# Two-layer AdaLN network on one core: the third sequence's rotary projections moved from attention groups 0 to 2 into the lead-in

## The chip, the core and the metric

The kernel runs on one core of one Trainium2 chip. The metric is device time in microseconds (us) of one execution. The engines are TensorE (PE, matmul; PEld is its weight load), VectorE (DVE), ScalarE (ACT), GpSimd (POOL) and SyncE (SP), which only issues DMAs here. Each engine works through its own instructions in order and waits on semaphores.

## What is computed

Four sequences of 512 tokens and 128 channels pass two AdaLN layers. Layer 0 is a Mamba-2 mixer and a dense run of 8 experts; layer 1 is causal attention with rotary positions and a routed MLP with the chosen expert of each token. The change touches the attention of layer 1 alone, which is, cut to what matters:

```python
q = (x @ W_q.T).reshape(B, S, 16, 8).transpose(0, 2, 1, 3)   # B = 4 sequences (two of them in name), S = 512
k = (x @ W_k.T).reshape(B, S, 16, 8).transpose(0, 2, 1, 3)
v = (x @ W_v.T).reshape(B, S, 16, 8).transpose(0, 2, 1, 3)
q, k = apply_rope(q), apply_rope(k)      # o1 = x1*cos - x2*sin, o2 = x1*sin + x2*cos
scores = einsum('bhqd,bhkd->bhqk', q, k) / sqrt(8)
probs = softmax(where(causal, scores, -inf))
attn = einsum('bhqk,bhkd->bhqd', probs, v)
x = x + ga * (attn @ W_o.T)
```

## The kernel before

**Projections.** For sequence b four projections are made, j = 0 to 3: q, q with neighbouring channels swapped, k, and k swapped. `project(b, j)` is one float32 product over the 512 tokens on PE, which the profile shows as two MATMULs of line 1876. `rope(b, j)` multiplies its result by cosine or sine on DVE (line 1309). `rotate` on POOL (line 560) adds two of these to a rotated q or k. ACT and POOL then split it into three bfloat16 parts (`part_hi` and `part_mid`, lines 869 and 873; `rest` and `last_part`, lines 566 and 571). SP stores the parts in DRAM (`parts_out`, line 366) and reads them back in another layout (`relayout`, line 378).

**Groups.** Attention runs over 16 groups of 4 heads, numbered by `it`, four groups to a sequence. Each group has 8 slots, i = 0 to 7. Work is staged: while group `it` makes its transposed scores (`scores_T`, lines 1973 and 1978), its exponentials on ACT (`probs`, line 882) and its weighted values (`weighted_values`, line 1992), the same slots make the plain scores of group `it + 2` on PE (`scores`, line 1900), of which DVE takes row maxima (`maximum`, line 1332). In slot 3 the maxima of group `it + 1`, split into parts by POOL (`max_parts`, lines 610 to 616), are transposed (`maxima_T`, line 1957), copied by ACT (line 967) and put into rows of `qaug` by four DMAs on SP (line 437); `scores_T` of the next group waits for these.

**The lead-in.** The loop begins with `it = -1`, which has no transposed scores and no exponentials: PE makes only plain scores of group 1 and, in slot 3, the maxima's transposes for group 0. Group 0 also carries the last residual of layer 0 and its statistics (lines 1910, 1315, 475 and 480) and a layer norm on DVE (line 494); group 1 carries four transposes for it (`x3_T`, line 1917).

**The ring.** Plain scores, projections and the small transposes share three PSUM banks in turn, in the order in which PE makes them. Before PE writes a bank it waits until the reader of what stood there three items earlier (DVE, or ACT) is done. The order is built by the same loop as PE's and DVE's programs, so a projection that moves takes its place in the ring with it.

The table `ROPE_AT` gives the group in whose slots each projection stands; `ropes_at` adds the slot. Sequence 2's projections are first needed by POOL's `rotate` in group 1.

Of the kernel before, what the change touches and what calls it, by code (L numbers as in the profile page):

```python
# [72 lines left out]
def adaln_kernel(nc, x_in, mod_in, mixw_in, moe0_in, attn_in, moe1_in, const_in, bconst_in, kones_in, out):  # L73
    with ExitStack() as ctx:
# [203 lines left out]
                units.append(parts)  # L278
                maxima_done.append(maxima_done[-1] + len(parts))

        ROPE_AT = {(2, 0): 0, (2, 1): 1, (2, 2): 2, (2, 3): 2, (3, 0): 4, (3, 1): 5, (3, 2): 6, (3, 3): 6}

        def ropes_at(it, i):

            return [bj for bj, at_it in ROPE_AT.items() if at_it == it and i == (1 if bj[1] == 2 else 5)]

        def parts_at(it):

# [24 lines left out]
        for it in range(-1, 16):  # L313
            for i in range(8):
                if it + 2 < 16:
                    for n in at_slot[i]:
                        ring.append((("mx", it + 2, n), ("mx", 16 * (it + 2) + maxima_done[n + 1])))
                if i == 3 and 0 <= it + 1 < 16:
                    ring.append((("mT", it + 1), ("mT", it + 2)))
                if i == 3 and 0 <= it - 1:  # L320
                    ring.append((("oT", it - 1), ("at", it)))
                if i == 5 and it >= 4 and it % 4 == 0:
                    ring.append((("aT", it // 4 - 1), ("aT", it // 4)))
                if i == 7 and it >= 4 and it % 4 == 0:
                    ring.append((("ao", it // 4 - 1), ("x3", it // 4)))
                for b, j in ropes_at(it, i):
                    ring_projection(b, j)
                if it in (4, 8) and i == 6:
                    ring_projection((it + 4) // 4, 4)
                if (it, i) == (0, 1):  # L330
                    ring.append((("y0T", B - 1), ("x2", B)))
                if (it, i) == (1, 1):
                    ring.append((("x3T", B - 1), ("hT", 3 * B)))
                if (it, i) in ROUTER_AT:
                    what = ROUTER_AT[it, i]
                    ring.append((what, {"h4T": ("hT", 3 * B + what[1] + 1), "logits": ("logits", what[1] + 1),
                                        "ranks": ("ranks", what[1] + 1)}[what[0]]))
# [663 lines left out]
        def _(v):  # L1001
# [513 lines left out]
            for it in range(-1, 16):  # L1515
                for i in range(8):
                    if (it, i) == (0, 3):
                        residual(B - 1)
                    if (it, i) == (0, 7):
                        ln_apply(v, 3, x, xn, B - 1)  # L1520
                    if it + 2 < 16:
                        for u in at_slot[i]:
                            maximum(it + 2, u)
                    if i == 3 and 0 <= it - 1:
                        o_norm(it - 1)
                    if i == 7 and it >= 4 and it % 4 == 0:
                        attn_out(it // 4 - 1)
                    for b, j in ropes_at(it, i):
                        rope(b, j)
                    if it >= 5 and it % 4 == 1 and i in (2, 4):  # L1530
                        router_input(it // 4 - 1, i // 2 - 1)
                    if (it, i) == (14, 5):
                        logits_in(0)
                        choose(0)
                    elif (it, i) == (14, 7):
                        positions(0)
                        second_best(0)
                    elif (it, i) == (15, 4):
                        logits_in(1)
                        choose(1)  # L1540
                    elif (it, i) == (15, 7):
                        positions(1)
                        early_table()
                        second_best(1)
# [90 lines left out]
        def _(pe):  # L1635
# [412 lines left out]
            for it in range(-1, 16):  # L2048
                if it == 0:
                    pe.wait_ge(sem("pr"), DENSE)  # L2050
                for i in range(8):
                    if it + 2 < 16:
                        for u in at_slot[i]:
                            scores(it + 2, u)
                    if 0 <= it < 16:
                        scores_T(8 * it + i)
                    if i == 3 and 0 <= it + 1 < 16:
                        maxima_T(it + 1)
                    if i % 2 == 1 and 0 <= 4 * it + i // 2 - 1 < 64:
                        weighted_values(4 * it + i // 2 - 1)  # L2060
                    if i == 3 and 0 <= it - 1:
                        o_T(it - 1)
                    if i == 5 and it >= 4 and it % 4 == 0:
                        a_T(it // 4 - 1)
                    if i == 7 and it >= 4 and it % 4 == 0:
                        attn_out(it // 4 - 1)
                    for b, j in ropes_at(it, i):
                        project(b, j)
                    if it in (4, 8) and i == 6:
                        project_values((it + 4) // 4)  # L2070
                    if (it, i) == (0, 1):
                        y0_T(B - 1)
                    if (it, i) == (1, 1):
                        x3_T(B - 1)
                    if (it, i) in ROUTER_AT:
                        what, n = ROUTER_AT[it, i]
                        router_step[what](n)
# [172 lines left out]
```

## Time and profile before

| | us |
|---|---|
| median of 3 runs | 541.46 (540.17 to 542.07) |
| the profiled execution | 538.46 |
| its span, first to last instruction | 536.5 |
| PE busy | 455.4 (85%) |
| DVE busy | 396.8 (74%) |
| ACT busy | 280.6 (52%) |
| mean granted TensorE clock | 0.927 |

The profiled execution's own time is 3.00 us under the median and 1.96 us over its span. The granted clock is given as a share of full speed: 1.00 is 2.4 GHz and 0.50 is 1.2 GHz. Attention takes the stretch from about 287 us to 444 us of the span.

### The profile page before, as it was taken

What the parts mean: (1) busy time and instruction counts of PE and PEld (TensorE: products, weight loads), DVE (VectorE), ACT (ScalarE), POOL (GpSimd) and SP (SyncE); (2) the same over time, 40 slices, a digit from 0 to 9 for tenths busy, and PEclk for the clock granted to TensorE, in tenths of its full rate; (3) what the DMA queues carried; (4) which work ended last, traced back from release to release, by engine and by line L of the source; (5) the groups of instructions that cost most, each with busy time, mean ns of one, the idle gap of its engine ahead of it and who ended that gap; (6) DMA issues with size and microseconds to landing.
All of it is one profiled execution on the core that took longest, in us unless ns stands there. A gap on an engine that the chain in (4) does not pass through costs nothing.

```text
span 536.5 us, 10400 instructions
## 1 busy us (share of the span) xinstructions
PE 455.4 (85%) x3156; PEld 275.7 (51%) x3156; DVE 396.8 (74%) x1328; ACT 280.6 (52%) x525; POOL 235.6 (44%) x332
## 2 busy tenths in 40 slices
PE   4798778987898999979996899999999997588990
PEld 4664557765653444435332344534545453587990
DVE  5899848889535689778898789888899636445544
ACT  3569986653443444443542578677678753112330
POOL 4210048999300387765843124034065536032760
PEclk9989899999789899989997799999999978579996
DMA  8991000000001532247760003214255101112115
GB/s 350 360 384 37 1 1 2 1 2 0 9 0 53 109 105 84 68 136 197 207 146 2 3 4 90 62 33 135 78 168 182 62 17 46 26 48 74 53 45 166
DMA packets 31471, 47.58 MB, mean 89 GB/s; under 512 B 3709, under 2 KB 21437, under 8 KB 30509
## 3 DMA queue, kind: packets, MB, share of 16 engines
q1 hardware_dynamic: 29448, 43.99, 27.0%
q0 software_dynamic: 1248, 2.59, 1.5%
q8 instruction: 27, 0.44, 0.4%
q10 hardware_dynamic: 720, 0.34, 0.3%
q14 instruction: 28, 0.22, 0.1%
HBM read 27.59 MB, written 19.12 MB: 87 GB/s over the span
## 4 chain that ended last, share of the span: by engine, by line
PE 44%; DVE 16%; issue 9%; POOL 5%; DMA 5%; SPq 4%; ACT 3%; DVEq 0%; POOLq 0%; ACTq 0%
PE ps L1992 6%; DVE arena L1332 4%; PE ps L1928 3%; PE ps L2098 3%; PE ps L1930 3%; PE ps L1876 3%; PE ps L2107 3%; PE ps L1865 3%; PE ps L1978 3%; PE ps L1900 2%; PE ps L1791 2%; DMA arena<-expert_weights 2%; PE ps L1973 1%; DVE arena L1301 1%; POOL slots_x L674 1%
## 5 line engine op out<-in xcount | busy, mean ns | idle before, releaser
L1332 DVE CUSTOM_DVE_ANT_0 arena<-ps,const 128x512 bf16<-128x512 f32 (+3 forms) x256 | 110.8, 486 | 7.7 <-PE ps L1900 7.4
L882 ACT ACTIVATE arena<-ps 128x256 f32<-128x256 f32 (+3 forms) x128 | 85.2, 703 | 38.5 <-PE ps L1978 37.8
L592 POOL TENSOR_TENSOR arena<-arena 128x512 f32<-128x512 f32 x32 | 45.7, 1428 | 63.4 <-DVE arena L1301 63.3
L1900 PE MATMUL ps<-arena 48*128 48x128 bf16 (+3 forms) x256 | 51.6, 310 | 8.8 <-DVE arena L1332 6.6
L1992 PE MATMUL ps<-arena 128*32 128x512 f32 (+3 forms) x512 | 51.0, 464 | 0.4 <-ACT arena L882 0.4
L1978 PE MATMUL ps<-arena 51*128 51x128 bf16 (+3 forms) x256 | 49.0, 310 | 0.0
L1973 PE MATMUL ps<-bconst 64*128 64x64 bf16 x512 | 42.9, 195 | 2.0 <-DMA arena<-arena 1.9
L1900 PEld LDWEIGHTS ps<-arena 48*128 48x128 bf16 x256 | 17.1, 95 | 53.2 <-DVE arena L1332 31.0
L909 ACT ACTIVATE arena<-arena 128x512 f32<-128x512 f32 x32 | 20.1, 629 | 43.8 <-DVE arena L1301 43.0
L1928 PE MATMUL ps<-arena,moe 128*128 128x512 f32 x64 | 35.8, 642 | 5.7 <-DVE arena L1284 5.6
L952 ACT ACTIVATE arena<-ps 128x512 f32<-128x512 f32 x23 | 13.7, 598 | 45.4 <-PE ps L2098 45.4
L1973 PEld LDWEIGHTS ps<-bconst 64*128 64x128 bf16 x512 | 29.4, 97 | 11.2 <-DMA arena<-arena 3.0
L1930 PE MATMUL ps<-arena,moe 128*128 128x512 f32 x64 | 34.2, 618 | 0.0
L682 POOL DMA_INDIRECT tokens_y<-arena,token_at x23 | 22.5, 980 | 26.4 <-DVE token_at L1563 16.1
L1111 DVE SCALAR_TENSOR_TENSOR arena<-ps,mixw,arena 128x511 f32<-128x511 f32 (+2 forms) x48 | 33.1, 740 | 0.9 <-ACT arena L752 0.9
L1865 PE MATMUL ps<-arena,moe 128*128 128x512 f32 x64 | 32.8, 594 | 0.0
L1284 DVE TENSOR_TENSOR arena<-hT,arena 128x512 f32<-128x512 f32 x32 | 24.8, 774 | 9.7 <-DMA arena<-expert_weights 9.7
L1292 DVE SCALAR_TENSOR_TENSOR arena<-ps,moe,arena 128x512 f32<-128x512 f32 x32 | 23.9, 747 | 9.7 <-PE ps L1930 9.3
L2098 PE MATMUL ps<-arena 128*128 128x128 f32 x184 | 27.0, 294 | 3.0 <-DVE arena L1556 2.5
L529 POOL TENSOR_TENSOR arena<-arena 128x256 f32<-128x256 f32 x16 | 12.4, 774 | 37.0 <-ACT arena L745 33.3
L674 POOL DMA_INDIRECT slots_x<-rows,posu x16 | 15.8, 988 | 27.9 <-DVE posu L1445 20.9
L2107 PE MATMUL ps<-arena 128*128 x184 | 26.5, 293 | 0.0
(268 smaller groups left out, 1081.6 us busy)
## 6 DMA issues: line engine op xcount, KB each, us to landing
slots_x<-arena SPq DMA_DIRECT2D x1, 8910.0 KB, 39.4
arena<-expert_weights SPq DMA_DIRECT2D x32, 256.0 KB, 4.0
qk_parts<-arena SPq DMA_DIRECT2D x48, 128.0 KB, 2.4
arena<-qk_parts SPq DMA_DIRECT2D x52, 96.0 KB, 2.4
arena<-moe_in SPq DMA_DIRECT2D x4, 1025.0 KB, 5.4
moe<-moe_in SPq DMA_DIRECT2D x1, 1936.0 KB, 14.2
arena<-slots_x SPq DMA_DIRECT2D x18, 66.0 KB, 1.9
arena<-qk_parts SPq DMA_DIRECT2D x4, 288.0 KB, 5.8
```

Source lines behind the costliest of these rows:

```text
L592: pool.tensor_tensor(yacc[:, ts], yacc[:, ts], pr[:, i % 2, :], ALU.add).then_inc(sem("yacc"), 1)
L882: act.activation(pt[:, u % 4, :, 0:n], ps[:, 4 + 2 * k:6 + 2 * k, 0:n], ACT.Exp, scale=ATT_SCALE).then_inc(sem("probs"), 1)
L1332: v.tensor_tensor_reduce(out=junk[:, done % 2, 0:n], in0=ps[:, k, col:col + n], in1=w["mask"][:, (3 - qt) * P:4 * P], scale=1.0, scalar=3 ...
L1865: pe.matmul(ps[:, 6 + i % 2, :], w["w2"][:, e * D:(e + 1) * D], gT[:, i % 2, :], start=True, stop=True).then_inc(sem("p2_ps"), 1)
L1900: mm = pe.matmul(ps[:, k, col:col + n], qaug[lo:lo + KR, b % 2, 2 * g + j // 2, qt * P:(qt + 1) * P], kaug[lo:lo + KR, b % 2, 2 * g + j // ...
L1928: pe.matmul(ps[:, 2 + i % 2, :], w["w1"][:, e * D:(e + 1) * D], xm[:, i % 2, :], start=True, stop=True).then_inc(sem("p1_ps"), 1)
L1930: pe.matmul(ps[:, 4 + i % 2, :], w["w3"][:, e * D:(e + 1) * D], xm[:, i % 2, :], start=True, stop=True).then_inc(sem("p3_ps"), 1)
L1973: pe.matmul(ps[:, bank, HALF * qh:HALF * (qh + 1)], w["causal"][lo:lo + HALF, qh * P:(qh + 1) * P], w["half"][lo:lo + HALF, :], start=(qh ...
L1978: mm = pe.matmul(ps[:, bank, 0:n], kaug[lo:lo + KM, b % 2, 2 * g + jp, kt * P:(kt + 1) * P], qaug[lo:lo + KM, b % 2, 2 * g + jp, kt * P:S] ...
L1992: mm = pe.matmul(ps[32 * j:32 * j + 32, 3, kt * P:S], va[:, b % 2, kt, 4 * (s % QG) + j, :], pt[:, (2 * m + j // 2) % 4, j % 2, 0:n], star ...
L2098: mm = pe.matmul(ps[:, 4 + n % 2, q * P:(q + 1) * P], w1[:, n % 2, q * P:(q + 1) * P], xT[:, n % 2, :], start=True, stop=True)
L2107: mm = pe.matmul(ps[:, 6 + n % 2, 0:D], gs[:, n % 2, q * P:(q + 1) * P], w["W2"][:, bass.ds(at_w[n] + q * D, D)], start=(q == 0), stop=(q ...
```

## The change

Sequence 2's four projections and the four DVE operations that read them move to `it = -1`, to slots 4, 5, 6 and 7 behind that slot's plain scores. Sequence 3's stay in groups 4 to 6. No instruction is added or removed.

```diff
--- before.py
+++ after.py
@@ -278,11 +278,11 @@
                 units.append(parts)
                 maxima_done.append(maxima_done[-1] + len(parts))
 
-        ROPE_AT = {(2, 0): 0, (2, 1): 1, (2, 2): 2, (2, 3): 2, (3, 0): 4, (3, 1): 5, (3, 2): 6, (3, 3): 6}
+        ROPE_AT = {(2, 0): -1, (2, 1): -1, (2, 2): -1, (2, 3): -1, (3, 0): 4, (3, 1): 5, (3, 2): 6, (3, 3): 6}
 
         def ropes_at(it, i):
 
-            return [bj for bj, at_it in ROPE_AT.items() if at_it == it and i == (1 if bj[1] == 2 else 5)]
+            return [bj for bj, at_it in ROPE_AT.items() if at_it == it and i == (bj[1] + 4 if it < 0 else 1 if bj[1] == 2 else 5)]
 
         def parts_at(it):
 
```

**PE, the lead-in.** The rows start with the four transposes of the maxima (line 1957, slot 3 of `it = -1`). The rows of line 1900 are plain scores, of line 1876 the projection, and lines 1973 and 1978 are the first transposed scores of group 0. Before:

```order
L1957 MATMUL ps<-bconst,arena 12x128 x4
L1900 MATMUL ps<-arena 128x256 x4
L1900 MATMUL ps<-arena 128x512 x2
L1900 MATMUL ps<-arena 128x384
L1900 MATMUL ps<-arena 128x128
L1900 MATMUL ps<-arena 128x384
L1900 MATMUL ps<-arena 128x128
L1900 MATMUL ps<-arena 128x512
L1973 MATMUL ps<-bconst 128x64 x4
L1978 MATMUL ps<-arena 128x128 x2
```

Now:

```order
L1957 MATMUL ps<-bconst,arena 12x128 x4
L1900 MATMUL ps<-arena 128x256 x2
L1876 MATMUL ps<-hT,attn 128x512
L1900 MATMUL ps<-arena 128x256 x2
L1876 MATMUL ps<-hT,attn 128x512
L1900 MATMUL ps<-arena 128x512 x2
L1876 MATMUL ps<-hT,attn 128x512
L1900 MATMUL ps<-arena 128x384
L1900 MATMUL ps<-arena 128x128
L1900 MATMUL ps<-arena 128x384
L1900 MATMUL ps<-arena 128x128
L1876 MATMUL ps<-hT,attn 128x512
```

A projection now stands behind each of the four slots' plain scores, and all four stand ahead of group 0's first `scores_T`.

**DVE, the lead-in.** The rows start at slot 5; line 1332 is the row maximum, in two instructions, and line 1309 the multiplication by cosine or sine. Before:

```order
L1332 ISA arena<-ps,const 128x256
L1332 ISA arena 128x1
L1332 ISA arena<-ps,const 128x256
L1332 ISA arena 128x1
L1332 ISA arena<-ps,const 128x512
L1332 ISA arena 128x1
L1332 ISA arena<-ps,const 128x512
L1332 ISA arena 128x1
L1332 ISA arena<-ps,const 128x384
L1332 ISA arena 128x1
L1332 ISA arena<-ps,const 128x128
```

Now:

```order
L1309 TENSOR_TENSOR arena<-ps,const 128x512
L1332 ISA arena<-ps,const 128x256
L1332 ISA arena 128x1
L1332 ISA arena<-ps,const 128x256
L1332 ISA arena 128x1
L1309 TENSOR_TENSOR arena<-ps,const 128x512
L1332 ISA arena<-ps,const 128x512
L1332 ISA arena 128x1
L1332 ISA arena<-ps,const 128x512
L1332 ISA arena 128x1
L1309 TENSOR_TENSOR arena<-ps,const 128x512
L1332 ISA arena<-ps,const 128x384
```

Each multiplication stands between the maxima of one slot and those of the next.

**PE, from slot 7 of group 1 to slot 2 of group 2.** Lines 1973 and 1978 are transposed scores, line 1992 the weighted values (the row with 384 columns is slot 7's, the one with 512 columns slot 1's). Before:

```order
L1973 MATMUL ps<-bconst 128x64 x4
L1978 MATMUL ps<-arena 128x512 x2
L1992 MATMUL ps<-arena 32x384 x4
L1900 MATMUL ps<-arena 128x512
L1973 MATMUL ps<-bconst 128x64 x4
L1978 MATMUL ps<-arena 128x128 x2
L1900 MATMUL ps<-arena 128x512
L1973 MATMUL ps<-bconst 128x64 x4
L1978 MATMUL ps<-arena 128x128 x2
L1992 MATMUL ps<-arena 32x512 x4
L1876 MATMUL ps<-hT,attn 128x512
L1900 MATMUL ps<-arena 128x384
```

Now:

```order
L1973 MATMUL ps<-bconst 128x64 x4
L1978 MATMUL ps<-arena 128x512 x2
L1992 MATMUL ps<-arena 32x384 x4
L1900 MATMUL ps<-arena 128x512
L1973 MATMUL ps<-bconst 128x64 x4
L1978 MATMUL ps<-arena 128x128 x2
L1900 MATMUL ps<-arena 128x512
L1973 MATMUL ps<-bconst 128x64 x4
L1978 MATMUL ps<-arena 128x128 x2
L1992 MATMUL ps<-arena 32x512 x4
L1900 MATMUL ps<-arena 128x384
```

The projection behind slot 1's weighted values is gone. The other three leave the same kind of gap: one in slot 5 of each of the groups 0, 1 and 2. The rows around them keep their order. ACT's, POOL's and SP's programs keep their order.

## Rows read from the trace of the kernel before

**Rows 1.** The page: busy time, share of the span, instructions.

```profile
PE 455.4 (85%) x3156; PEld 275.7 (51%) x3156; DVE 396.8 (74%) x1328; ACT 280.6 (52%) x525; POOL 235.6 (44%) x332
```

**Rows 2.** Windows from slot 2 to the next group's slot 1: groups 1, 2, 3.

```profile
core 0: us, PE busy (x) PEld busy (x) DVE busy (x) ACT busy (x) POOL busy (x), PEclk, DMA share, GB/s
...
306.97:316.62 9.65, 9.07 (x111) 4.31 (x111) 8.25 (x36) 6.98 (x11) 2.33 (x7) 1.00 0.01 3
316.62:326.85 10.23, 9.65 (x112) 4.20 (x112) 8.59 (x37) 7.40 (x12) 4.42 (x8) 1.00 0.24 64
326.85:334.61 7.76, 7.54 (x107) 3.69 (x108) 7.42 (x36) 7.04 (x12) 3.23 (x7) 1.00 0.23 63
```

**Rows 3.** Timeline of PE, 305 to 312 us.

```profile
305.90 1.07 PE L1992 MATMUL ps<-arena 128*32 128x512 f32 x8
306.89 0.66 PE L1917 MATMUL ps<-const,rows 128*128 128x128 f32 x4
```

**Rows 4.** Timeline of PE, 315 to 335 us.

```profile
315.56 1.06 PE L1992 MATMUL ps<-arena 128*32 128x512 f32 x8
316.55 1.13 PE L1876 MATMUL ps<-hT,attn 128*128 128x512 f32 x2
...
321.26 1.12 PE L1876 MATMUL ps<-hT,attn 128*128 128x512 f32 x2
...
333.54 1.07 PE L1992 MATMUL ps<-arena 128*32 128x512 f32 x8
```

**Rows 5.** Timeline of PE around the lead-in's end; idle time in brackets.

```profile
287.00 0.40 PE L1900 MATMUL ps<-arena 48*128 48x256 bf16 x4
287.74 3.10 PE L1900 MATMUL ps<-arena 48*128 48x512 bf16 x7 [0.35 <-ACT arena L967]
291.79 0.29 PE L1973 MATMUL ps<-bconst 64*128 64x64 bf16 x4 [0.95 <-DMA arena<-arena]
```

**Rows 6.** Timeline of DVE in the lead-in and group 0.

```profile
287.43 0.42 DVE L1332 CUSTOM_DVE_ANT_0 arena<-ps,const 128x256 bf16<-128x256 f32 x1 [0.57 <-PE ps L1900]
...
291.47 0.69 DVE L1332 CUSTOM_DVE_ANT_0 arena<-ps,const 128x512 bf16<-128x512 f32 x1
...
301.79 0.69 DVE L1309 TENSOR_TENSOR arena<-ps,const 128x512 f32<-128x512 f32 x1 [2.52 <-PE ps L1876]
```

**Rows 7.** Chain that ended last: start, us, what.

```profile
289.99 1.75 DMA arena<-arena
...
299.89 1.87 PE ps L1876 x2
```

**Rows 8.** Busy time and granted clock in windows of 1 us, 287 to 302.

```profile
287.00:288.00 1.00, 0.65 (x7) 0.20 (x5) 0.57 (x3) 0.88 (x2) 0.00 (x0) 0.91 0.00 0
...
291.00:292.00 1.00, 0.21 (x8) 0.21 (x10) 1.00 (x5) 0.00 (x0) 0.34 (x2) 0.50 0.03 11
...
295.00:296.00 1.00, 0.27 (x4) 0.07 (x2) 0.96 (x5) 0.87 (x2) 0.00 (x0) 0.50 0.00 0
...
300.00:301.00 1.00, 1.00 (x2) 0.33 (x2) 0.00 (x0) 0.00 (x0) 0.00 (x0) 0.50 0.01 3
301.00:302.00 1.00, 1.00 (x10) 0.20 (x8) 0.21 (x1) 0.00 (x0) 0.00 (x0) 0.76 0.00 0
```

**Rows 9.** The same around an earlier fall of the clock.

```profile
175.00:176.00 1.00, 1.00 (x2) 0.30 (x2) 0.58 (x1) 0.97 (x2) 0.00 (x0) 0.59 0.59 170
...
178.00:179.00 1.00, 1.00 (x3) 0.41 (x2) 0.00 (x0) 0.69 (x1) 0.00 (x0) 0.70 0.95 131
```

**Rows 10.** Windows: DVE's group 0; PE's group 0 and two slots more.

```profile
292.10:306.10 14.00, 12.43 (x111) 5.73 (x111) 9.84 (x47) 6.61 (x11) 1.70 (x4) 0.67 0.01 3
...
291.79:306.97 15.18, 13.61 (x120) 6.12 (x121) 11.02 (x49) 6.90 (x11) 2.55 (x8) 0.68 0.01 2
```

**Rows 11.** Timeline of the SP queue: DMA issues.

```profile
322.52 3.84 SPq L366 DMA_DIRECT2D qk_parts<-arena  x6
328.96 2.82 SPq L437 DMA_DIRECT2D arena<-arena  x4
```

## The prediction

> **What bounds the kernel now.** I read the page first: PE is busy for 455.4 us, 85% of the span, DVE for 74%, ACT for 52% [rows 1]. That average says little about one stretch, so the next view is the busy time in windows, cut where slot 1's weighted values end on PE. Those ends are 305.90 + 1.07 = 306.97 [rows 3], 315.56 + 1.06 = 316.62 and 333.54 + 1.07 = 334.61 [rows 4]. The reader is to see three consecutive groups that differ in little but the projections [rows 2]. From group 1 to 2 it takes 9.65 us, with one projection; from 2 to 3 it takes 10.23 us, with two; from 3 to 4 it takes 7.76 us, with none. In the last, PE is busy 7.54 us of 7.76 and DVE 7.42. Both are nearly full, PE a little more, so a projection taken out of PE's stream should shorten the group.
>
> The timeline of the lead-in's end shows something else. PE makes the last plain scores of the lead-in in 3.10 us from 287.74, paced by DVE, and stands idle 0.95 us before group 0's first `scores_T` at 291.79. It waits for the DMAs that bring the maxima's rows [rows 5], whose last wait in the chain is 1.75 us long [rows 7]. The third view is the granted clock. It falls from 1.00 to 0.50 (1.2 GHz) within 287 to 288 and returns within 301 to 302 [rows 8]. In between, PE has two thin microseconds, 291 to 292 (0.21 busy) and 295 to 296 (0.27 busy). Group 0 thus runs at half clock for most of its length: PE needs 15.18 us from 291.79 to 306.97, at a mean clock of 0.68 [rows 10]. DVE's idle time there is PE's doing: before its multiplication at 301.79 it waits 2.52 us for the projection [rows 6].
>
> **Groups 1 and 2 lose three projections.** The 7.76 us without a projection is the base. The window from group 1 to 2 holds `x3_T` besides, four transposes in 0.66 us [rows 3], of which 0.63 us is taken as their cost: 9.65 - 7.76 - 0.63 = 1.26 us for its one projection. The next holds two: 10.23 - 7.76 = 2.47 us, 1.24 us each. The two MATMULs of one take 1.13 or 1.12 us on PE [rows 4], so the groups show them at full price with a small wait besides. The gain is 1.26 + 2.47 = **3.73 us**. It needs DVE not to become the bound, and the 7.76 us group shows that it can follow at that pace with its 7.42 us of work [rows 2]. The rotated sums on POOL get their inputs earlier than they ask for them. On SP the stores of the parts (3.84 us from 322.52) stand ahead of the next maxima's rows at 328.96 [rows 11]; they leave 2.6 us in the queue, and taking out slot 5's 1.24 us shortens that and does not use it up. If it did, `scores_T` of group 3 would start late by what is missing, which I bound at 1 us.
>
> **The lead-in gets four projections.** Here they run at half clock. One took 1.87 us in the chain at 299.89, at a granted 0.50 [rows 7, 8]. If a projection's time were only that of full clock, 1.13 us, four would cost 4.5 us; at 1.87 us they cost 7.5 us. For the plain scores I take the four matmuls of 256 columns at full clock, 1024 columns in 0.40 us [rows 5]. The seven that follow have 2560 columns (two of 512, two of 384, two of 128, one of 512), so 1.0 us at full and 2.0 us at half clock; their 3.10 us was DVE's pace. PE's sum from 287.40 is then 2.0 + 7.5 = 9.5 us, and `scores_T` starts at 296.9 if the clock stays at half, 5.1 us later than 291.79. The 0.95 us of idle time is within that.
>
> The Trainium skill ("TensorE: Matmul & The Clock Gate", Part 1) says that back-to-back matmuls take just twice as long at 1.2 GHz, less a fixed 2.5 ns. By that an uncovered projection would cost 2 x 1.13 = 2.26 us in place of the row's 1.87 us, an estimate, and the lead-in 1.6 us more. The row decides, as 1.13 us holds a latency that doesn't double.
>
> **The clock.** With the projections PE has no thin microsecond from about 287.2 on. At the earlier fall within 175 to 176 PE stayed at 1.00 busy, and the clock was back within 178 to 179, 3 us later [rows 9]. In the lead-in it took nearly 14 us, with the two thin stretches [rows 8]. So I expect the rise 3 to 7 us after 287.8, at 291 to 295. At 295 PE has done about 7.2 of the 9.5 us; the other 2.3 take half as long, and `scores_T` starts at about 295.5, 3.7 us late. At 291 three projections are still to come, DVE sets the pace and it starts at about 294.1, 2.3 us late.
>
> **Group 0 is given back by DVE's limit.** Once the clock is up, PE's own work in group 0 would fit in about 7 us: 7.76 less slot 1's weighted values of 1.07, which group 0 doesn't have. DVE can't follow. Its window from 292.10 to 306.10 holds 9.84 us of work, of which 0.69 is the multiplication that leaves, so 9.15 us remain [rows 6, 10]. In the lead-in DVE works from 287.43 and starts group 0's first maximum at 291.47, which takes 0.69 us [rows 6]. With the multiplications, the last of which waits for the last projection, I get that maximum's end at 296.7 for the late rise and at 295.9 for the early one. Adding 9.15 gives 305.9 and 305.0 against 306.10. DVE never runs without a gap; its idle share in the 7.76 us window (0.34 of 7.76, 4.4%) adds 0.4 us, so 306.3 and 305.4. The middle is 305.9: lead-in and group 0 together gain **0.2 us**. The late start is paid by the 1.87 us projection gone from group 0, the waits behind it, and the clock.
>
> **The sum.** 3.73 + 0.2 = 3.9 us. Behind group 3 the order of work is as before and shifts as a whole. Against the profiled execution's own time that is 538.46 - 3.9 = 534.6 us. The median of the runs is 3.0 us above that execution, so for the median I say 541.46 - 3.9 = **537.5 us**. A measurement of this kernel tells about 0.3%, 1.6 us, from no change.
>
> **The rivals.**
>
> *A larger gain.* The clock rises early and nothing idles on DVE: 305.0 against 306.10 in group 0, and the 3.73 us: 4.8 us, 536.6. If the fall of the clock shifts too and does not cover the whole lead-in, another microsecond comes off: 535.6.
>
> *The clock rises no sooner than before, at 301.5.* `scores_T` starts at 296.9. Before, 291.79 to 301.68 held the projection of 1.87 us and 8.0 us of the rest. After, 4.6 us of that are done by 301.5, and 3.4 us run at full clock in 1.7 us, so that point is reached at 303.2, 1.5 us late. Gain 3.73 - 1.5 = 2.2 us: 539.3. For it speaks that the stretch from 292 to 295 raised nothing; against it, that it had a thin microsecond on either side. The same page of the Trainium skill warns that the length of the slow stretch varies from run to run. By that rule the early rise can't be counted on.
>
> *The work is only moved.* The lead-in pays 5.1 us, all at half clock, and group 0 gives back its projection's 1.87 us and nothing of the clock, since DVE holds it: 5.1 - 1.87 = 3.2 us lost against 3.73 won. That is a gain of 0.5 us: 541.0, no change.
>
> *Slower.* The clock stays down through the lead-in and group 0 and into group 1, because DVE is the limit there and PE waits for ring banks. From 301.5 on each microsecond of half clock costs 0.5 us. The gain of 2.2 us is gone at 306, and the kernel is slower by 1.6 us if the rise comes after 309. Up to the end of group 1, about 315, it costs 0.5 x 13.5 = 6.8 us: 541.46 + 4.6 = 546.1. Against it speaks that at half clock PE is itself the bound, and then dense, as from 296 to 301.
>
> **Chances and range.** The forecast, 536.5 to 538.8, has 0.50. The larger gain has 0.12, the unchanged rise 0.18 (two thirds of it under 539.8), the moved work 0.12, slower 0.08. Faster by over 0.3% is 0.50 + 0.12 + 0.12 = 0.74; within it is 0.12 + 0.06 = 0.18; slower is 0.08. The range for 8 in 10 leaves out the slower case and part of the two outermost: 535.4 to 541.0.
>
> **What would show it.** In the profile after: the distances between slot 1's weighted values should be about 8.4, 7.76 and 7.76 us. Line 1973 should first appear at 294 to 296.5. The half clock should end by 295. In group 0 DVE should be busy above 90%, with PE waiting for line 1332. PE's wait of 0.95 us for the maxima's rows should be gone. The prediction is wrong if the half clock lasts to 300 or beyond, if the distance from group 2 to 3 stays above 8.5 us, or if a second low stretch opens behind group 0.

## The result, and the profile after

The changed kernel takes **539.49 us** in the median of 22 runs (533.64 to 546.57, and one far off at 845.85) against 542.05 us before (22 runs, 536.32 to 546.52). The ratio is **0.994**, with an interval of 0.9917 to 0.9964; it leaves out the executions that are over 1.5% above the fastest of their kernel, five of these 22 and among them the profiled one. A second set of 12 timed runs gave 0.9967 (0.9928 to 1.0006), whose interval includes no change. So the change gains 0.3% to 0.6%, 2 to 3 us; forecast were 3.9 us and 0.993.

The profiled execution took 546.26 us, so I read a second one beside it (`after_again`, 539.39 us). First the groups. These are the windows of that second profile from the end of slot 1's weighted values to the next one's (busy time of each engine, then clock, share of DMA, GB/s), groups 1 and 2; before they took 9.65 and 10.23 us [rows 2]:

```profile
309.15:317.62 8.47, 8.05 (x112) 4.15 (x112) 7.58 (x35) 6.93 (x11) 2.29 (x7) 1.00 0.01 3
317.62:325.38 7.76, 7.53 (x107) 3.65 (x108) 7.42 (x36) 7.03 (x12) 4.15 (x7) 1.00 0.17 46
```

They now take 8.47 and 7.76 us, and 7.76 is the length of a group without projections. The first profile shows 7.76 us for group 2 as well, and 8.93 us for group 1, which begins at half clock.

Then the lead-in. This is PE's timeline in the second profile. The maxima's transposes start at 286.86 and the projections are the rows of line 1876:

```profile
286.86 0.50 PE L1957 MATMUL ps<-bconst,arena 128*12 128x128 bf16 x4 [1.38 <-DVE arena L1332]
287.29 0.60 PE L1900 MATMUL ps<-arena 48*128 48x256 bf16 x2
287.83 2.07 PE L1876 MATMUL ps<-hT,attn 128*128 128x512 f32 x2
289.83 0.60 PE L1900 MATMUL ps<-arena 48*128 48x256 bf16 x2
290.37 2.07 PE L1876 MATMUL ps<-hT,attn 128*128 128x512 f32 x2
292.37 0.61 PE L1900 MATMUL ps<-arena 48*128 48x512 bf16 x2
293.22 2.08 PE L1876 MATMUL ps<-hT,attn 128*128 128x512 f32 x2 [0.24 <-DVE arena L1309]
295.23 0.61 PE L1900 MATMUL ps<-arena 48*128 48x384 bf16 x4
296.08 1.68 PE L1876 MATMUL ps<-hT,attn 128*128 128x512 f32 x2 [0.24 <-DVE arena L1309]
...
301.14 0.33 PE L1957 MATMUL ps<-bconst,arena 128*12 128x128 bf16 x3 [0.82 <-DVE x L1315]
```

Here [rows 5] is answered. There is no wait for the DMAs any more: the first transposed scores start at 297.70, 10.84 us behind the transposes, where it was 5.11 us (286.68 to 291.79). Each of the first three projections takes 2.07 or 2.08 us. In this view the reader is to see where the two waits of 0.24 us come from, DVE's multiplication of the projection before, and that PE waits for little else. The waits for line 1315 (0.82 us) come in group 0 and are DVE's.

The clock in windows of 1 us, in the first profile:

```profile
288.00:289.00 1.00, 0.57 (x5) 0.36 (x6) 0.61 (x4) 0.09 (x1) 0.30 (x2) 0.59 0.00 0
...
293.00:294.00 1.00, 1.00 (x2) 0.00 (x0) 0.00 (x0) 0.00 (x0) 0.00 (x0) 0.50 0.01 3
...
299.00:300.00 1.00, 1.00 (x6) 0.24 (x6) 0.23 (x3) 0.00 (x0) 0.64 (x3) 0.50 0.00 0
...
301.00:302.00 1.00, 1.00 (x9) 0.61 (x10) 0.77 (x4) 0.28 (x2) 0.00 (x0) 0.59 0.00 0
...
303.00:304.00 1.00, 0.27 (x9) 0.30 (x12) 0.97 (x3) 0.47 (x1) 0.00 (x0) 1.00 0.00 0
...
305.00:306.00 1.00, 0.38 (x5) 0.34 (x6) 1.00 (x7) 0.73 (x1) 0.92 (x2) 0.62 0.00 0
...
311.00:312.00 1.00, 1.00 (x11) 0.33 (x9) 0.98 (x8) 0.20 (x1) 0.00 (x0) 0.50 0.00 0
...
315.00:316.00 1.00, 1.00 (x19) 0.60 (x17) 0.16 (x1) 0.58 (x2) 0.00 (x0) 0.76 0.00 0
```

It falls within 288 to 289 and returns within 301 to 302, after nearly 14 us as before [rows 8], though PE is busy for 1.00 us in most of these microseconds. It then falls again within 305 to 306 for 10 us, behind 303 to 304, where PE is busy 0.27 us. The second profile has one stretch only:

```profile
286.00:287.00 1.00, 0.14 (x3) 0.14 (x4) 1.00 (x8) 0.53 (x1) 0.65 (x3) 1.00 0.00 0
...
290.00:291.00 1.00, 1.00 (x3) 0.50 (x2) 1.00 (x4) 0.00 (x0) 0.00 (x0) 0.50 0.02 6
...
297.00:298.00 1.00, 1.00 (x10) 0.26 (x10) 0.62 (x5) 0.00 (x0) 0.43 (x2) 0.88 0.00 0
298.00:299.00 1.00, 0.78 (x15) 0.59 (x12) 1.00 (x2) 0.66 (x2) 0.44 (x2) 1.00 0.00 0
```

It begins at 287 and ends within 297 to 298. My forecast for the end was 291 to 295.

Group 0 is the last place. These are the windows from its first transposed scores to the end of slot 1's weighted values of group 1, in the second profile; the third number is DVE's busy time:

```profile
297.70:309.15 11.45, 8.88 (x120) 4.29 (x120) 11.08 (x49) 6.88 (x11) 2.55 (x8) 1.00 0.01 3
```

DVE is busy for 11.08 of 11.45 us, 97%, and PE for 8.88. At full clock DVE does hold group 0, as forecast. Before it took 15.18 us, with DVE busy for 11.02.

### The profile page after: what moved, and what is told of

It reads as the page before. It is cut to its first block, busy times and chain, and to the rows that moved or that the text cites. A ratio compares the mean times of both kernels' runs of the same rounds, so it can differ in the third digit from the quotient of the medians.

```text
span 544.4 us, 10400 instructions
## 1 busy us (share of the span) xinstructions
PE 460.2 (85%) x3156; PEld 277.6 (51%) x3156; DVE 396.2 (73%) x1328; ACT 280.0 (51%) x525; POOL 235.4 (43%) x332
## 4 chain that ended last, share of the span: by engine, by line
PE 44%; DVE 18%; issue 10%; POOL 5%; DMA 4%; SPq 3%; ACT 2%; DVEq 0%; POOLq 0%; ACTq 0%
PE ps L1992 5%; DVE arena L1332 5%; PE ps L1876 4%; PE ps L1928 3%; PE ps L2107 3%; PE ps L1930 3%; PE ps L2098 3%; PE ps L1865 3%; PE ps L1900 3%; PE ps L1978 2%; PE ps L1791 2%; DMA arena<-expert_weights 2%; DVE arena L1301 1%; PE ps L1973 1%; POOL slots_x L674 1%
## 5 line engine op out<-in xcount | busy, mean ns | idle before, releaser
L1928 PE MATMUL ps<-arena,moe 128*128 128x512 f32 x64 | 34.0, 613 | 6.4 <-DVE arena L1284 6.3
L1865 PE MATMUL ps<-arena,moe 128*128 128x512 f32 x64 | 32.8, 594 | 0.0
L1930 PE MATMUL ps<-arena,moe 128*128 128x512 f32 x64 | 32.7, 592 | 0.0
L610 POOL CAST arena<-arena 128x16 bf16<-128x16 f32 x16 | 3.4, 213 | 60.6 <-DVE arena L1332 60.6
L2098 PEld LDWEIGHTS ps<-arena 128*128 128x128 f32 x184 | 24.4, 207 | 6.5 <-DVE arena L1556 5.8
```

The lines of the kernel that those rows point to most:

```text
L1865: pe.matmul(ps[:, 6 + i % 2, :], w["w2"][:, e * D:(e + 1) * D], gT[:, i % 2, :], start=True, stop=True).then_inc(sem("p2_ps"), 1)
L1928: pe.matmul(ps[:, 2 + i % 2, :], w["w1"][:, e * D:(e + 1) * D], xm[:, i % 2, :], start=True, stop=True).then_inc(sem("p1_ps"), 1)
L1930: pe.matmul(ps[:, 4 + i % 2, :], w["w3"][:, e * D:(e + 1) * D], xm[:, i % 2, :], start=True, stop=True).then_inc(sem("p3_ps"), 1)
L2098: mm = pe.matmul(ps[:, 4 + n % 2, q * P:(q + 1) * P], w1[:, n % 2, q * P:(q + 1) * P], xT[:, n % 2, :], start=True, stop=True)
```

## The experiments

All profiles are laid side by side first. "Scores" is the time from the maxima's transposes (line 1957) to group 0's first transposed scores (line 1973). "Group 0" goes on from there to the end of slot 1's weighted values of group 1. "All" is the time from the start of the last expert product (line 1865) to slot 1's end in group 3, beyond which nothing differs. "Half clock" is the shortfall of the granted clock in windows of 0.5 us between 280 and 320, counted double: the time at 0.50, rounded to whole us. The last column is the timed ratio to the kernel before. All columns but that one come from a single profile of each kernel.

| run | scores | group 0 | 1 to 2 | 2 to 3 | all | half clock | ratio |
|---|---|---|---|---|---|---|---|
| before | 5.11 | 15.18 | 9.65 | 10.23 | 45.37 | 14 | 1 |
| before_again | 5.30 | 15.34 | 9.66 | 10.22 | 45.72 | 17 | |
| after | 11.33 | 14.64 | 8.93 | 7.76 | 47.85 | 24 | 0.994 |
| after_again | 10.84 | 11.45 | 8.47 | 7.76 | 43.72 | 10 | 0.9967 |
| none | 5.34 | 14.81 | 8.46 | 7.76 | 41.58 | 20 | 0.9933 |
| early | 5.14 | 14.75 | 8.47 | 7.76 | 42.40 | 14 | 0.996 |
| before_fill | 5.31 | 14.20 | 9.65 | 10.23 | 44.59 | 3 | 0.9998 |
| after_fill | 7.95 | 13.38 | 8.47 | 7.76 | 42.76 | 7 | 0.9926 |
| early_fill | 5.93 | 11.28 | 8.48 | 7.76 | 40.11 | 0 | 0.9871 |
| early_fill_again | 5.92 | 11.29 | 8.47 | 7.76 | 40.10 | 0 | 0.9877 |
| early_fill_more | 5.93 | 11.30 | 8.47 | 7.75 | 40.10 | 0 | 0.9879 |
| dummy | 7.44 | 12.57 | 9.67 | 10.22 | 45.09 | 3 | 1.0048 |
| fill_narrow | 7.30 | 13.02 | 8.46 | 7.76 | 41.74 | 7 | 0.9887 |
| pair | 6.84 | 14.90 | 8.46 | 10.22 | 45.62 | 17 | 1.0039 |

**Both kernels again.** No edit.

before_again: 

> The kernel before, unchanged, for a second profile of it. If the half-clock stretch that begins in the lead-in is a matter of how dense PE's work is, as the prediction has it, it starts near 287 us and lasts 10 us or more again, and the groups 1 to 3 take 9.65, 10.23 and 7.76 us again. If its place and length are set by chance, it will be shifted by several us or be absent.

after_again: 

> The changed kernel, unchanged, for a second profile and more timings. The prediction's theory (a dense lead-in brings the clock back early) expects half clock to end within 7 us of its start and 0.993 of the time before. The rival (the clock rises no sooner) expects the 13.7 us of the first profile again and 0.994 to 0.998. If the second low stretch of that profile, 10.2 us in groups 0 and 1, belongs to the change, it will be there again; if it was chance, it won't.

Before, the groups take the same to 0.01 us, and the half clock is there again, 17 us long in place of 14. Of the changed kernel's two profiles, one has 24 us of it and one 10. In all four it starts in the lead-in; how long it lasts differs between executions of one kernel. The expected early return did not come in either. The second low stretch is no fixed part of the change.

**none: sequence 2's projections left out.**

```diff
-        ROPE_AT = {(2, 0): 0, (2, 1): 1, (2, 2): 2, (2, 3): 2, (3, 0): 4, ...
+        ROPE_AT = {(3, 0): 4, ...
```

(The counts that POOL and DVE wait for are lowered to match.)

> The kernel before without sequence 2's four projections and their four DVE multiplications: they are left out altogether, and its rotated q and k are made from what stands in the buffers. It prices all four where they stood. My sum says 1.26 + 2.47 us in groups 1 and 2 and 1.87 us plus waits of about 1 us in group 0: 6.6 us less than before, a ratio of 0.988. What this run has over the changed kernel is what the four cost in the lead-in: 2.7 us by my sum; 3 us or more if the lead-in pays them at half clock in full (about 6 if nothing there hides); near 0 if they lie in PE's wait.

0.9933 (0.9898 to 0.9968), 3.6 us, and not 6.6. The groups gave what was expected: 9.65 and 10.22 us became 8.46 and 7.76, 3.65 us together. Group 0 gave next to nothing, 14.81 us for 15.18 to 15.34, with its half clock at 20 us. Leaving the four out thus measures about as moving them did. The two differ by 0.0007 to 0.0034, within their intervals, so this run can't price the lead-in by times. By the profiles it is 41.58 us against 43.72 and 47.85, with 20 us of half clock against 10 and 24.

**early: the projections in the slots 0 to 3.**

```diff
-            return [... i == (bj[1] + 4 if it < 0 else 1 if bj[1] == 2 else 5)]
+            return [... i == (bj[1] if it < 0 else 1 if bj[1] == 2 else 5)]
```

> The changed kernel with the four projections in the slots 0 to 3 of the lead-in instead of 4 to 7. PE has idle time of 0.41, 0.25, 0.88 and 1.38 us there and still runs at full clock. If the clock falls because PE is thin in these slots, it stays up or falls later, and the time is 2 to 4 us under the changed kernel's (ratio to before 0.986 to 0.990). If DVE sets the pace there, its 2.5 us come ahead of the first exponentials all the same, the maxima's rows for group 0 leave later, and the time is that of the changed kernel within 1 us.

0.996 (0.9923 to 0.9996), no better than the changed kernel in time, though its profile is better: the projections run at full clock, in 1.12 us, in what had been PE's waits. PE's timeline:

```profile
283.41 1.12 PE L1876 MATMUL ps<-hT,attn 128*128 128x512 f32 x2 [0.24 <-DVE arena L1332]
...
284.78 1.13 PE L1876 MATMUL ps<-hT,attn 128*128 128x512 f32 x2
...
286.16 1.12 PE L1876 MATMUL ps<-hT,attn 128*128 128x512 f32 x2
...
287.54 0.39 PE L1957 MATMUL ps<-bconst,arena 128*12 128x128 bf16 x4
288.07 1.12 PE L1876 MATMUL ps<-hT,attn 128*128 128x512 f32 x2
```

The transposes start 6.28 us behind the last expert product in place of 5.20, and the first transposed scores 5.14 us behind them. So four projections cost 1.1 us there, at full clock, against 5.5 to 6.2 us in the slots 4 to 7 at half clock (and 2.6 at full clock, as `after_fill` shows below). The clock fell later, at 293, behind the slots 4 to 7, which were thin now (0.70 busy from 290 to 291), and stayed down 14 us, nearly all of it in group 0. That fits thin slots as the reason for the fall. But the time is not the 0.986 to 0.990 that I expected of a clock that falls later.

**Fillers: keeping PE busy.** In three kernels PE gets bfloat16 matmuls of 448 columns that nobody reads.

```diff
+            def fill(n):
+                for _ in range(n):
+                    pe.matmul(ps[:, 4, 0:448], identb, bconst[:, :], start=True, stop=True)
+            FILL = [0, 2, 2, 4, 5, 0, 2, 2]      # before_fill, and 5 ahead of group 0
+            FILL = [0, 2, 2, 4, 5, 0, 0, 0]      # after_fill
+            FILL = [0, 0, 0, 2, 3, 1, 2, 3]      # early_fill, and 5 ahead of group 0
             for it in range(-1, 16):
                 for i in range(8):
+                    if it < 0:
+                        fill(FILL[i])
```

before_fill: 

> The kernel before with 22 extra bfloat16 matmuls of 448 columns on PE, in the gaps of the lead-in (2, 2, 4, 5, 0, 2, 2 in the slots 1 to 7 and 5 ahead of group 0); their results are read by nobody. They keep PE busy where it was thin. If thin stretches of PE bring the clock down there, it stays at 1.00 through the lead-in and group 0, the stretch from the first transposed scores to slot 1 of group 1 takes 10.5 to 12 us in place of 15.2, and the run takes 0.992 to 0.995 of the time before. If the fall comes anyway, that stretch stays at 14 us or more and the ratio is 1.000 to 1.004.

after_fill: 

> The changed kernel with 13 of these fillers, in the slots 1 to 4 of the lead-in alone; the projections fill the rest. At full clock I expect each projection in the lead-in to take 1.1 us of PE in place of 2.1, the first transposed scores 7 us behind the maxima's transposes in place of 11, and a ratio of 0.986 to 0.990. It should beat the kernel before with fillers by 2 to 3 us if the groups' gain is real at full clock, since then DVE is what holds the lead-in and group 0. If the rest of the gain was lost to the wait of group 0 for DVE and not to the clock, it equals the changed kernel.

early_fill: 

> The projections in the slots 0 to 3, and 16 fillers (2 in slot 3, 3, 1, 2 and 3 in the slots 4 to 7, 5 ahead of group 0). In the run without fillers the clock fell at 293.2, behind the thin slots 4 to 7. If these cause it, the half clock is gone and the ratio is 0.984 to 0.989, the lowest of all. If not, it is that of the run without fillers, 0.996.

In none of the three did the clock fall in the lead-in; before, it had in every profile without fillers except the one of `early`, where the projections filled it. But it gave the kernel before no time that could be measured: 0.9998 (0.9962 to 1.0034), against 0.992 to 0.995 expected of a clock that stays up throughout. It did not stay up throughout: group 0 took 14.20 us for 15.18, with 3 us of half clock in it. PE's timeline in its group 0, at full clock up to 298:

```profile
296.98 0.33 PE L1957 MATMUL ps<-bconst,arena 128*12 128x128 bf16 x3 [0.82 <-DVE x L1315]
...
298.87 0.39 PE L1900 MATMUL ps<-arena 48*128 48x256 bf16 x1 [0.74 <-DVE arena L1332]
...
300.84 1.85 PE L1876 MATMUL ps<-hT,attn 128*128 128x512 f32 x2
```

PE waits 0.82 us for DVE's residual and 0.74 us for its maxima. These waits are themselves followed by a fall of the clock, within 298 to 299, and the projection at 300.84 takes 1.85 us again.

`after_fill` measured 0.9926 (0.9893 to 0.9958), 3.9 us less than `before_fill` by the ratios (0.0072 of 541). I had expected 0.986 to 0.990 and a lead of 2 to 3 us. The 3.9 us equal my forecast for the change, but the two profiles don't bear that out: over the stretch they differ by 1.8 us (44.59 and 42.76), 3.65 us gained in the groups and 1.8 lost ahead of them. What the other 2 us of the timed difference are isn't shown. The projections take 1.12 us, and the first transposed scores come 7.95 us behind the transposes: 2.6 us later than in `before_fill`, where the changed kernel without fillers had them 5.5 to 6.2 us late.

```profile
286.94 1.12 PE L1876 MATMUL ps<-hT,attn 128*128 128x512 f32 x2
...
288.32 1.12 PE L1876 MATMUL ps<-hT,attn 128*128 128x512 f32 x2
...
290.23 1.13 PE L1876 MATMUL ps<-hT,attn 128*128 128x512 f32 x2 [0.30 <-DVE arena L1309]
...
292.13 1.13 PE L1876 MATMUL ps<-hT,attn 128*128 128x512 f32 x2 [0.30 <-DVE arena L1309]
...
296.73 0.33 PE L1957 MATMUL ps<-bconst,arena 128*12 128x128 bf16 x3 [0.82 <-DVE x L1315]
```

`early_fill` measured **0.9871** (0.982 to 0.9923). That is what I expected of it (0.984 to 0.989). Its profile has no half clock between 280 and 320 at all; group 0 takes 11.28 us, of which DVE is busy for 11.02.

**dummy: PE's share of the lead-in alone.**

```diff
+                    if it < 0 and i >= 4:
+                        pe.matmul(ps[:, 4, :], w["wq"], hT[:, 0:S], start=True, stop=True)
```

> The kernel before with four more projection matmuls (W_q times the first sequence, results read by nobody) in the slots 4 to 7 of the lead-in, on PE alone, without DVE's multiplications. It prices PE's share of the lead-in. At full clock four take 4.3 us, and 0.95 us of it fills the wait: 3.4 us late, ratio 1.006. At half clock they take 8 us and the first transposed scores come about 11 us behind the maxima's transposes in place of 5.1, as in the changed kernel, ratio 1.008 to 1.011. If they come much sooner than in the changed kernel, DVE's four multiplications had a share in that delay.

1.0048 (1.0004 to 1.0092), near the case of full clock. (Of its ten timed runs one is far off, at 1445.08 us, and not counted.) Four such products in the lead-in made the kernel 2.6 us slower, though in this profile, of its fastest execution, the clock came back fast and the stretch is no longer than before (45.09 us). PE's timeline:

```profile
284.44 0.39 PE L1957 MATMUL ps<-bconst,arena 128*12 128x128 bf16 x4 [1.39 <-DVE arena L1332]
...
285.08 1.60 PE L2070 MATMUL ps<-hT,attn 128*128 128x512 f32 x2
...
287.14 2.04 PE L2070 MATMUL ps<-hT,attn 128*128 128x512 f32 x2
...
289.43 1.13 PE L2070 MATMUL ps<-hT,attn 128*128 128x512 f32 x2
...
290.81 1.12 PE L2070 MATMUL ps<-hT,attn 128*128 128x512 f32 x2
...
295.11 0.33 PE L1957 MATMUL ps<-bconst,arena 128*12 128x128 bf16 x3 [0.82 <-DVE x L1315]
```

The first two ran at half clock (1.60 and 2.04 us), the last two at full (1.13 and 1.12). So the clock can come back in about 3 us in a dense lead-in, as I had forecast it for the changed kernel, where it took 10 and 14 us. The difference can't be put down to the waits of 0.24 us for DVE there: in `after_again` the clock falls at 287 and the first of them comes at 292.98, 6 us later, with the clock still at 0.50. `pair` below says the same.

Group 0 with its projection, all at full clock, takes 12.57 us here, and 15.18 or 15.34 us before. So the half clock costs the kernel before some 2.7 us in group 0. Without the projection it is 11.3 to 11.5 us: at full clock the projection costs 1.1 to 1.3 us there.

**Repeats and one more filler.** `early_fill_more` has four fillers more, in slot 3 of group 0 ahead of the transposes.

early_fill_again: 

> The kernel with the projections in the slots 0 to 3 and 16 fillers, again, since its ratio of 0.987 rests on six runs. If it is real, 0.985 to 0.990 again and a profile without the long half-clock stretch at the lead-in; if six runs flattered it, 0.990 to 0.994.

early_fill_more: 

> The same with four more fillers in slot 3 of group 0, ahead of the maxima's transposes, where PE waits 0.82 us for DVE's residual. If the thin stretches of PE that DVE's limit leaves in group 0 bring the clock down there in a part of the executions, its median is 0.5 to 2 us under the other's. If not, both are the same within 0.5 us.

0.9877 (0.9838 to 0.9916) and 0.9879 (0.9844 to 0.9915), again without half clock, and 40.10 us in both. So the gain is real, 6.6 us by the ratios, of which this stretch shows 5.3 to 5.6 (45.37 and 45.72 before). The extra fillers do nothing.

**fill_narrow: DVE's share.** In `after_fill`, sequence 2's multiplications work on 64 tokens only.

```diff
+                n = 64 if b == 2 else S
-                v.tensor_tensor(ropet[:, j, :], ps[:, k, :], w[("cos", "sin")[j % 2]], ALU.mult)\
+                v.tensor_tensor(ropet[:, j, 0:n], ps[:, k, 0:n], w[("cos", "sin")[j % 2]][:, 0:n], ALU.mult)\
```

> The changed kernel with 13 fillers, and sequence 2's four multiplications on DVE over 64 of the 512 tokens only; the rest of its rotated q and k is made from what stands in the buffers. It takes about 0.5 us off each of four operations. If DVE is what holds the lead-in and group 0 at full clock, as the prediction has it, the way from the maxima's transposes to slot 1 of group 1 is 1.5 to 2 us shorter than with fillers alone (21.3 us, with 6.8 us of half clock in it). If PE holds it, it is the same within 0.5 us.

From the transposes to slot 1 of group 1 it takes 20.32 us against 21.33, with 7 us of half clock in both: 1.0 us less, between the two expectations. In the lead-in itself it is 7.30 against 7.95. That fits a bound which PE and DVE share; with one profile of each it is not more than that. The time, 0.9887 (0.9845 to 0.9929), is lower than that of `after_fill` by 2 us, within the intervals.

**pair: half of the change.**

```diff
-        ROPE_AT = {(2, 0): -1, (2, 1): -1, (2, 2): -1, (2, 3): -1, (3, 0): 4, ...
+        ROPE_AT = {(2, 0): -1, (2, 1): -1, (2, 2): 2, (2, 3): 2, (3, 0): 4, ...
```

> The change by half: (2, 0) and (2, 1) in the lead-in's slots 4 and 5, (2, 2) and (2, 3) left in group 2. The distance from group 1 to 2 is 8.4 us, as in the changed kernel, and from 2 to 3 10.2 us, as before. At half clock two projections make the lead-in about 3.5 us longer than before (8.6 us from the maxima's transposes to the first transposed scores in place of 5.1 and about 11). If a gain were proportional, the ratio is 0.997. If the 0.95 us wait and the queue of DVE hide more of the first two than of the last, it is 0.994 or less.

1.0039 (1.0002 to 1.0076): slower than before, where every theory had a gain. The groups did as expected, 8.46 and 10.22 us. Scores took 6.84 us, 1.5 to 1.7 late and not the 3.5 that I expected at half clock. PE's timeline and the clock in windows of 1 us:

```profile
283.72 0.39 PE L1900 MATMUL ps<-arena 48*128 48x256 bf16 x2
284.04 1.93 PE L1876 MATMUL ps<-hT,attn 128*128 128x512 f32 x2
285.90 0.60 PE L1900 MATMUL ps<-arena 48*128 48x256 bf16 x2
286.44 1.71 PE L1876 MATMUL ps<-hT,attn 128*128 128x512 f32 x2
```

```profile
284.00:285.00 1.00, 1.00 (x4) 0.36 (x2) 0.78 (x4) 0.98 (x2) 0.00 (x0) 0.61 0.00 0
286.00:287.00 1.00, 1.00 (x3) 0.52 (x3) 0.99 (x4) 0.00 (x0) 0.00 (x0) 0.50 0.01 3
287.00:288.00 1.00, 1.00 (x2) 0.00 (x0) 0.38 (x4) 0.00 (x0) 0.00 (x0) 0.68 0.01 4
```

The clock falls within 284 to 285 and is back within 287 to 288, some 3 us later. Up to there PE's order is that of the changed kernel, and neither kernel has a wait in it. So the same work was followed by an early return here and in `dummy`, and by a late one in both profiles of the changed kernel. How dense PE is does not decide it alone.

The clock fell again at 291 for 14 us, and group 0 took 14.90 us, though one projection had left it. Under half clock, taking that one out is worth 0.3 to 0.4 us (15.18 and 15.34 before). So the lead-in's two were paid in full, and group 1's 1.2 us was nearly the whole gain. By the profiles that is even, 45.62 us against 45.37 and 45.72.

**The clock of the timed runs.** One profile of a kernel says little about a clock that differs between executions. The record also has the mean granted clock of every timed run. These are the means for each kernel (without the two runs far off), beside the kernel before in the same set:

| run | clock | before, same set |
|---|---|---|
| after_again | 0.933 | 0.930 |
| none | 0.928 | 0.930 |
| early | 0.933 | 0.930 |
| before_fill | 0.939 | 0.931 |
| after_fill | 0.939 | 0.931 |
| early_fill, _again, _more | 0.946, 0.947, 0.946 | 0.931 |
| dummy | 0.935 | 0.931 |
| fill_narrow | 0.943 | 0.931 |
| pair | 0.926 | 0.931 |

In the first set the changed kernel had 0.934. So the fillers keep the clock up in the timed runs too, and `pair` has the lowest clock of all. Within the runs of one kernel, 0.01 of this clock goes with 3 to 4 us of time (a line through the 29 runs of the kernel before in each of two sets, and through the changed kernel's 21 and 12). By that estimate the 0.005 of `pair` are 1.5 to 2 us, about what the profiles leave unexplained, and the 0.003 by which the changed kernel is above the kernel before are about 1 us of its gain. Why the clock of `pair` is lower isn't shown.

## Why the prediction was right, and where it was off

**Groups 1 and 2: right.** Forecast 3.73 us, measured 9.65 + 10.23 - 8.47 - 7.76 = 3.65 us, and to 0.02 us the same in every kernel with all four moved or left out whose group 1 began at full clock. (In the first profile group 1 began at half clock and took 8.93 us: 3.19 us.) Reading a projection's price from groups that differ in nothing else was the firmest step.

**Lead-in: mis-sized.** I had the first transposed scores 2.3 to 3.7 us late, and 5.1 us if the clock stayed at half. They were 5.7 and 6.2 us late. Three things add up. The clock came back within 297 to 298 and 301 to 302, not at 291 to 295. A projection at half clock took 2.00 us from its start to that of the next scores (287.83 to 289.83), where I had 1.87 us from one row of the chain [rows 7]; four make 0.5 us. And PE waited twice 0.24 us for DVE's multiplications, which I had put at nothing. The sum for the late rise also has a slip: with 2.3 us left at 295, at half the time, it gives 296.2 and not 295.5, 4.4 us late and not 3.7.

The page of the Trainium skill that I had weighed against that row ("TensorE: Matmul & The Clock Gate", Part 1) gave an estimate of 2.26 us. The measured 2.00 lies between the two. From start to start a projection takes 1.06 us at full clock (286.94 to 288.00 in `after_fill`), so half clock takes 1.9 times as long here and not twice; the measurement decides.

**The clock: the step that failed.** That PE without a thin microsecond gets the clock back 3 to 7 us after the fall was wrong in both profiles of this kernel (about 10 and 14 us), and right in `dummy` and `pair` (3 us each), though PE's order up to the early return is the same in all four. The evidence for it was one earlier fall under float32 products of full height [rows 9]; the lead-in mixes those with scores of 48 rows. Two of the signs that I had named for a wrong prediction came in the first profile: the half clock lasted beyond 300, and a second low stretch opened in group 0 and reached group 1. The rival of the unchanged rise (0.18) has that profile's first rise, at 301.5, but a gain of 2.2 us with it; with a low stretch up to 315 the profile is nearer to the rival "slower" (0.08). Neither describes the second profile.

**Group 0: right.** I forecast that DVE holds it once the clock is up, busy for over 90%. It was busy for 97% in `after_again` and 98% in `early_fill`. With the clock up group 0 took 11.3 to 11.5 us, not 15.2, in the kernels without its projection; of these 3.8 us some 2.7 are the clock's and 1.1 to 1.3 the projection's, by `dummy`. That is why the late start of 5.7 us cost `after_again` only 2.0 and 1.65 us against the two profiles of before (22.29 us from the transposes to slot 1 of group 1, in place of 20.29 and 20.64).

**The sum.** For lead-in and group 0 I had a gain of 0.2 us. It was a loss of about 1.8 us in one profile and of 5.3 to 5.7 us in the other, where a second low stretch fell into group 0. Over the whole stretch the one profile gains 1.65 to 2.0 us (43.72 against 45.37 and 45.72), the other loses 2.1 to 2.5. The timed gain of 2 to 3 us lies at the better end or beyond. The time lies inside the range, but with 539.49 us not in the forecast's own 536.5 to 538.8; "faster" was right with half to four fifths of the size. That it came so near is in part luck: one of the two terms was wrong in sign, and the profiles account for 2.0 us at best.

**What stays open.** What decides how long the half clock lasts. It is 24 and 10 us in two executions of one kernel, and the timed runs of one kernel spread over 6 to 13 us in the sets of ten or more. All profiles also have 17 to 31 us of half clock ahead of 280 us, where the programs are the same, and another 14 to 24 us from the end of attention to 515 us. Both differ between profiles and hide effects under 2 us. And no kernel without the four projections was run with fillers, which would give the least that this stretch can take.

## What to carry to other kernels

Work that is moved keeps its time only if it runs at the same clock and in front of the same waiting engine: price it where it lands. Three of the projections cost 3.65 us in groups 1 and 2. All four cost 5.5 to 6.2 us in the lead-in's slots 4 to 7 at half clock, 2.6 us there at full clock, and 1.1 us in the slots 0 to 3, where PE was waiting anyway. And the two changes belong together here: fillers alone gave 0.9998, the early slots alone 0.996, both 0.987 to 0.988. Where a clock differs between executions of one kernel, compare the mean clocks of many timed runs, since one profile of each tells little of it.

## What was not expected of the hardware

A half-clock stretch can outlast a stretch of nearly unbroken PE work. In the first profile PE was busy from 289 to 300 but for two waits of 0.24 us, and the granted clock was 0.50 throughout. The same order of PE's work, up to the second projection, was followed by full clock after 3 us in `pair`. PE's waits for DVE of 0.82 and 0.74 us within 2 us were followed by a fall in `before_fill`, and by none in `early_fill`, which has the same waits (0.82 and 0.75 us).
